# Cross-attention and routed experts on one core: softmax sums from ACT's accumulator in place of ones-matmuls

## The reference

```python
x = x + xattn(layernorm(x), ctx, ctx, mask, Wq, bq, Wk, bk, Wv, bv, Wo, bo)   # x, ctx: (8, 512, 512) fp32
x = x + ffn(layernorm(x), Ws, bs, W1, b1, W2, b2)

# xattn, 16 heads of 32
sim = einsum('bnid,bnjd->bnij', qh, kh) * 32 ** -0.5
sim = where(~mask[:, None, None, :], finfo.min, sim)
out = einsum('bnij,bnjd->bnid', softmax(sim, axis=-1), vh)      # then @ Wo + bo

# ffn: 8 experts, each takes the 512 tokens with the highest softmax(x @ Ws + bs)
h = gelu(einsum('ekd,edf->ekf', x[routes], W1) + b1)            # F = 2048
y = (einsum('ekf,efd->ekd', h, W2) + b2) * route_vals           # added back at routes
```

## Time and profile before

| | us |
|---|---|
| median of 3 runs | 1895.03 (1890.82 to 1898.14) |
| the profiled execution | 1893.99 |
| its span, first to last instruction | 1892.3 |
| TensorE busy (PE) | 1738.4 |
| VectorE busy (DVE) | 1145.1 |
| ScalarE busy (ACT) | 719.6 |
| GpSimd busy (POOL) | 459.2 |
| mean granted TensorE clock | 0.970 of full |

### The profile page before, as it was taken

One profiled execution on the slowest core, in us unless ns is written; L12 is line 12 of the kernel. 1 busy time (PEld: TensorE's weight loads), 2 busy tenths in 40 slices (PEclk: granted clock), 3 DMA queues, 4 the chain that ended last, 5 costly groups with the idle time before them and its releaser, 6 DMA issues.

```text
span 1892.3 us, 23403 instructions
## 1 busy us (share of the span) xinstructions
PE 1738.4 (92%) x8787; PEld 1171.3 (62%) x8787; DVE 1145.1 (61%) x1917; ACT 719.6 (38%) x1215; POOL 459.2 (24%) x730
## 2 busy tenths in 40 slices
PE   5799989989999999999899837999999999999996
PEld 4455645545546545455455325878888888888885
DVE  5576675775775865856766564777645454455543
ACT  3355454454554553543544511222223222222321
POOL 4332333323423323333333102010202020202001
PEclk9899999999999999999999957999999999999998
DMA  5232332323423323323323213243434242525331
GB/s 159 82 92 67 115 87 68 115 66 79 134 63 91 101 67 105 95 64 112 85 69 104 88 56 112 89 117 112 140 104 147 90 140 89 162 68 162 95 106 23
DMA packets 117289, 185.39 MB, mean 98 GB/s; under 512 B 24380, under 2 KB 58320, under 8 KB 117176
## 3 DMA queue, kind: packets, MB, share of 16 engines
q1 hardware_dynamic: 88312, 117.13, 19.5%
q0 software_dynamic: 28864, 66.75, 13.8%
HBM read 107.64 MB, written 25.31 MB: 70 GB/s over the span
## 4 chain that ended last, share of the span: by engine, by line
PE 76%; DVE 11%; issue 3%; DMA 3%; ACT 2%; SPq 2%; POOL 2%; ACTq 0%; POOLq 0%; DVEq 0%
PE ps_gen L635 8%; PE ps_gen L636 8%; PE ps_gen L637 8%; PE ps_gen L1643 6%; PE ps_gen L1645 6%; PE ps_gen L1644 6%; PE ps_den L1493 5%; PE ps_att L1493 5%; PE ps_gen L1465 5%; PE ps_gen L1479 4%; DVE maxes L1133 3%; PE ps_gen L1451 3%; PE ps_gen L1452 3%; PE ps_gen L1453 3%; DVE rden L1148 1%
## 5 line engine op out<-in xcount | busy, mean ns | idle before, releaser
L1133 DVE TENSOR_REDUCE maxes<-ps_gen 128x1 f32<-128x512 f32 x512 | 333.9, 675 | 203.0 <-PE ps_gen L1465 202.5
L948 ACT ACTIVATE p_ring<-ps_gen,keep_scale 128x512 f32<-128x512 f32 x512 | 331.8, 686 | 291.5 <-PE ps_gen L1479 291.2
L1350 DVE TENSOR_TENSOR gel_lo<-gel,gel_hi 128x512 fp32r<-128x512 f32 x126 | 87.2, 692 | 288.1 <-ACT gel_hi L1027 279.7
L1026 ACT ACTIVATE gel<-ps_gen,b_cols 128x512 f32<-128x512 f32 x128 | 88.3, 690 | 450.5 <-PE ps_gen L637 450.4
L1465 PE MATMUL ps_gen<-kst,qst 97*128 97x512 f32 x512 | 209.1, 428 | 23.0 <-issue 8.7
L1479 PE MATMUL ps_gen<-qst,kst 99*128 99x512 f32 x512 | 200.0, 436 | 17.6 <-DVE cT_lo L1083 9.0
L635 PE MATMUL ps_gen<-hT_hi,w_hi 128*128 128x512 f32 x512 | 203.0, 396 | 1.5 <-DVE hT_lo L1343 1.5
L636 PE MATMUL ps_gen<-hT_lo,w_hi 128*128 128x512 f32 x512 | 200.1, 391 | 0.0
L637 PE MATMUL ps_gen<-hT_hi,w_lo 128*128 128x512 f32 x512 | 200.1, 391 | 0.0
L1643 PE MATMUL ps_gen<-w_hi,gel_hi 128*128 128x512 f32 x504 | 198.1, 393 | 0.0
L895 POOL DMA_INDIRECT out_x<-y_out,idx x32 | 55.7, 1740 | 583.3 <-ACT y_out L1046 504.7
(11 more groups left out here) (199 smaller groups left out, 2778.4 us busy)
## 6 DMA issues: line engine op xcount, KB each, us to landing
w_raw<-in_L_ffn_W SPq DMA_DIRECT2D x128, 512.0 KB, 3.5
kst<-kT_hi POOLq DMA_DIRECT2D x256, 64.0 KB, 2.0
qst<-qT_hi SPq DMA_DIRECT2D x256, 64.0 KB, 2.0
x_in<-in_x POOLq DMA_DIRECT2D x60, 256.0 KB, 3.1
kst<-kT_lo POOLq DMA_DIRECT2D x128, 64.0 KB, 1.9
qst<-qT_lo SPq DMA_DIRECT2D x128, 64.0 KB, 2.0
out_x<-x_in SPq DMA_DIRECT2D x32, 256.0 KB, 2.0
hn_rows<-x_in SPq DMA_DIRECT2D x32, 256.0 KB, 2.1
```

Of the source, the lines that this page charges most:

```text
L948: e.activation(p_ring[n % NP_][:, :], ps("score", g, kt, h)[:, :], ACT.Exp, scale=keep_scale[:, b:b + 1]).then_inc(drained_sem("score", g, ...
L1133: e.reduce_max(maxes[:, h * TB + t:h * TB + t + 1], ps("max", g, h, t)[:, :], AX.X).then_inc(drained_sem("max", g, h, t), 1)
```

## The change

The softmax sums are made in another place. The max product of a tile is kept in its PSUM bank after DVE has taken its row extremes; ACT then takes exp(product - extreme) over the same tile, writes it back into the bank, and its accumulator output gives the row's sum in a column of `den` (step `sum`, 16 per group). The bank is free after that. So that the extreme can be ACT's bias, all is negated: Wq and its bias are multiplied by -SCALE when they are split, the products come out as the negated scaled scores, DVE takes a minimum into `nmax` (two buffers), and the exp has scale -1. `keep_scale` is 1 or 0 times -1.

The sums' way to the division: step `rden`, placed 0.02 into the next group: DVE reciprocal on 128x16, TensorE transpose to 16 rows, DVE copy into a part of `by_row`, a DMA of 8 KB on SP's queue to `rden_rows` in HBM; step `rden_in`, 0.3 into the next group: a DMA on SP's queue that reads it back with each head's row broadcast to 32 partitions, 256 KB into `rden_b`. DVE's `divide` multiplies `ps_att`, read in PSUM, by `rden_b`. The `den` steps, `ps_den`'s copies and the large reciprocals are gone; PSUM's eighth bank becomes a seventh `ps_gen`, which the search uses as `ps_den`. (Exp of the large product has the mask's row in it, as the scores have.)

The copies of V and route go from ACT to DVE. Of the table, V's products for the next batch are spread over one group's length from 0.36 of r3 on (`V_NEXT_AT`), the late work starts earlier and lasts 0.72 of a group for 0.52, and the context's loads are 0.1 of a group later. Waits on `s_av` count one step per kt where they counted two.

```diff
-NGEN = 6
+NGEN = 7
...
+    def max_of(self, g, h, t):
+        key = ("max", g, h, t)
+        self.with_bank(*key)
+        self.put_late(key, ("sum", g, h, t))
...
-    V_AT = (0.13, 0.33)
-    LOAD_C_AT, TURN_C_AT = (-0.1, 0.22), (0.5, 0.95)
+    RDEN_AT, RDEN_IN_AT = 0.02, 0.3
+    V_AT, V_NEXT_AT = (0.13, 0.33), (0.36, 1.36)
+    LOAD_C_AT, TURN_C_AT = (0.0, 0.32), (0.5, 0.95)
...
-    LATE_AT = (("residual", 0.15), ("add_bias", 0.38), ("out", 0.5), ("x1_norm", 0.61),
...
-    LATE_FOR = 0.52
+    LATE_AT = (("residual", 0.05), ("add_bias", 0.2), ("out", 0.3), ("x1_norm", 0.41),
...
+    LATE_FOR = 0.72
...
-            soon.extend([(a.add, "recip", g, n) for n in range(TB)] + [(a.add, "divide", g), (nothing,), (a.osplit, g)])
+            soon.extend([(a.add, "divide", g), (nothing,), (a.osplit, g)])
...
+                elif kind == "rden":
+                    g, = at
+                    on.wait_ge(*drained("rden", g))
+                    if g >= 2:
+                        on.wait_ge(s_rd_in, 16 * (g - 1))
+                    e.dma_start(rden_rows[g % 2].rearrange("h (t n) -> (h t) n", n=P), rd_rows).then_inc(s_rd_out, 16)
+
+                elif kind == "rden_in":
...
+                    src = rden_rows[g % 2].rearrange("h (r n) -> h r n", r=1).to_broadcast([HG, DH, S])
+                    e.dma_start(rden_b[:, :], src).then_inc(s_rd_in, 16)
...
-                    e.activation(w_hi[w][:, c, :], stage_of(w, c)[:, :], ACT.Copy).then_inc(s_w_hi, 1)
+                    e.activation(w_hi[w][:, c, :], stage_of(w, c)[:, :], ACT.Copy, scale=-SCALE if w == "q" else 1.0
...
+                elif kind == "sum":
+                    g, h, t = at
+                    c = slice(h * TB + t, h * TB + t + 1)
+                    psum = ps("max", g, h, t)
+                    on.wait_ge(s_min, (g * HG + h) * TB + t + 1)
+                    if g >= 2:
+                        on.wait_ge(s_rden, g - 1)
+                    e.activation(psum[:, :], psum[:, :], ACT.Exp, bias=nmax[g % 2][:, c], scale=-1.0, accum_out=den[g % 2][:, c]
+                                 ).then_inc(drained_sem("max", g, h, t), 1)
...
-                    e.activation(rden[:, :], ps_den[:, :], ACT.Copy).then_inc(s_nrm, 1)
-                    e.activation(att_n[:, :], ps_att[:, :], ACT.Copy).then_inc(s_nrm, 1)
...
-                    e.reduce_max(maxes[:, h * TB + t:h * TB + t + 1], ps("max", g, h, t)[:, :], AX.X
-                                 ).then_inc(drained_sem("max", g, h, t), 1)
+                    if g >= 2:
+                        on.wait_ge(*full("rows", g - 2))
+                        on.wait_ge(*drained("max", g - 2, HG - 1, TB - 1))
+                    e.tensor_reduce(nmax[g % 2][:, h * TB + t:h * TB + t + 1], ps("max", g, h, t)[:, :], AX.X, ALU.min
+                                    ).then_inc(s_min, 1)
...
+                    e.reciprocal(rden[:, :], den[g % 2][:, :]).then_inc(s_rden, 1)
+                    on.wait_ge(*full("rden", g))
+                    if g > 0:
+                        on.wait_ge(s_rd_out, 16 * g)
+                    e.tensor_copy(rd_rows, ps("rden", g)[0:HG * TB, 0:P]).then_inc(drained_sem("rden", g), 1)
...
+                    e.tensor_tensor(att_n[:, :], ps_att[:, :], rden_b[:, :], ALU.mult).then_inc(s_nrm, 1)
```

More of the change, by code:

```diff
@@ L310, in attention_agenda @@
             if before[0] >= 0:
[L311 removed]
+                attend(*before)
             fill(time[1])
[L313 to L314 removed]
             a.with_bank("score", i, kt, 2)
@@ L397, in attention_moe_kernel @@
         keep_scale = sb(p1, "keep_scale", [P, B])
-        maxes = sb(p1, "maxes", [P, HG * TB])
+        nmax = [sb(p1, f"nmax{i}", [P, HG * TB]) for i in range(2)]
+        den = [sb(p1, f"den{i}", [P, HG * TB]) for i in range(2)]
+        rden = sb(p1, "rden", [P, HG * TB])
         stat = [sb(p1, f"stat{i}", [P, 6]) for i in range(2)]
@@ L408, in attention_moe_kernel @@
         bias_rows = hnT[0:3 * DC, 2, :]
-        mask_neg = rden[0:B, :]
+        mask_neg = rden_b[0:B, :]
+        max_rows = [by_row[n * QUAD:n * QUAD + HG * TB, :] for n in range(2)]
+        rd_rows = raw(by_row[2 * QUAD:2 * QUAD + HG * TB, :])
         p1.close()
```

155 lines of the change are left out of this document (82 added, 73 removed).

## The result

The changed kernel takes 1959.6 us (median of 4 runs, 1948.4 to 1966.7); the kernel before took 1894.4 beside it. The ratio is 1.034, 95% interval 1.029 to 1.039: slower by 65 us, where 105 us less were forecast. The profiled execution is the shortest of the four and has a span of 1946.6 us; the two kernels differ by 54 us in their profiles.

The account below looks back on a forecast made before the run. TensorE was taken to bound attention. Seven batches at 13.5 us give 94.5, plus 4.7, 3.5 and 3.5 makes 106; 1894.0 - 106 + 1 = 1789 us, range 1757 to 1838.

Parts of the forecast that it names:

- A den step between other products takes 0.99 us ... 1.18 us ... 4.7 us per group: TensorE in attention: removing 128 ones-matmul steps at 1.18 us each saves 4.7 us per group, 151 us in all.
- the ones-matmuls were no bound: Rival, TensorE in attention: removed steps did not bound and the gain is eaten; 1894 us, from 1850 up; chance 0.04.
- The 45 us between those 151 and the forecast's 106: Whole kernel: den steps removed were priced at 151 us, but only 106 us of gain was forecast.
- r0: First of a batch's four kinds of group (four heads each): from 47.7 to 35.5 us, set by TensorE; ACT 24.
- r2: Third kind of group in a batch: from 24.35 to 23 us, ACT taking over from TensorE's 20.0.
- 1.1 us per batch for the banks held back: PSUM banks in attention: 1.1 of 14.6 us per batch kept back for max banks held by two instructions, leaving 13.5.
- I take 0.3 to 0.5 us each: TensorE early in the next group: wait for DVE at each of 32 added transposes of the reciprocals.
- It bounds nothing: DVE in attention: its busy time falls by 1 to 2 us per group and it limits no group.
- one fall per batch, 2.5 us, in a rival: Rival of held banks and clock: gaps lower TensorE's clock; with held banks, gain 7 us per batch, 1836 us; chance 0.14.
- nothing booked: Late work (residual to back), started earlier and spread wider: no cost counted, up to 3 us per batch for the range.
- r3: Fourth kind of group in a batch: from 25.8 to 29.7 us, TensorE gaining 8.3 us of V products.
- r1: Second kind of group in a batch: from 31.4 to 26.5 us, by TensorE with its 3.5 us idle kept.

Follow-up runs that it names:

- e13: Kernel before with three of four den steps (ones-matmuls) left out, nothing added or moved: 1861.6 us, ratio 0.982.
- e10: Changed kernel without ACT's sums and without the reciprocals' whole path, V and route copies back on ACT: 1814.7 us, ratio 0.957.
- e1: Changed kernel with rden moved from 0.02 to 0.3 of the next group and rden_in from 0.3 to 0.5: 1964.1 us, ratio 1.037.
- e6: Changed kernel with DVE's reciprocal left at 0.02, its transpose and copy moved to 0.25, the read to 0.45: 1956.6 us, ratio 1.033.
- e2: Changed kernel with only the route copies put back from DVE to ACT: 1944.0 us, ratio 1.026.
- e12: Changed kernel without ACT's sums and without the reciprocals' path, V and route copies staying on DVE: 1848.4 us, ratio 0.975.
- e7: Changed kernel with the old table's places for V, the context's loads and the late work: 2002.8 us, ratio 1.057.
- e16: Changed kernel with the sums' logarithm folded into the rows replacing the reciprocals' path, route copies on ACT, maxima, logarithm and rows placed earlier: 1909.1 us, ratio 1.007.

## Why the prediction was wrong

- **"A den step between other products takes 0.99 us ... 1.18 us ... 4.7 us per group": the first step that failed.** As work it was nearly right: 128 to 137 us of 151 left TensorE's account. As path it was not: with nothing added, 96 of the steps are worth 34 us and not 113 (e13), 0.35 us each. The argument was that TensorE, busy 94% of the stretch in rows 2, is the bound, so that what goes from it goes from the time. But 94% busy does not say how far the other chains are behind: at the place shown the stacks' chain already ended 0.64 us after TensorE did, so nothing of the step could come off there. The waits that grew in e13 are of three kinds (maxima 16 us, max products 11, layer norm 8.5), and the lower clock took 25 to 31 us more. The rival "the ones-matmuls were no bound" had 0.04, dismissed by those same 94%.
- **The 45 us between those 151 and the forecast's 106, for everything that was added: the second step that failed, and by more.** Sums, path and copies on DVE cost 145 us (e10 against the changed kernel). The prediction summed them as busy time per engine (24 of 35.5 us for ACT in r0), with 3 us in r2 for ACT and 1.1 us per batch for the banks held back. The runs show waits between the engines in place of that; the next two points are the parts that can be named.
- **"I take 0.3 to 0.5 us each" for the reciprocals' transpose: mis-sized.** It waited 57.8 us in 23 times, 2.5 us each. The row that it was sized by, the wait for the maxima, is a wait behind a max product; here DVE had the layer norm of two tiles ahead in the stop shown. But this wait alone is not the loss (e1, e6).
- **The route copies on DVE were costed as busy time only.** The logits wait for them, 35.9 us in 20 times; the engine of these copies is worth 16 us in e2, that of V's and route's together 34 us between e12 and e10. "It bounds nothing" was right for DVE's busy time (57% of the span, 1099.9 us where 1060 to 1090 was forecast) and wrong for its answers.
- **The clock was booked as one fall per batch, 2.5 us, in a rival.** It cost 59 to 69 us more than before in attention, some 8 per batch.
- **The late work's "nothing booked"** can't be told apart; its table as a whole helps (e7).
- **Right:** the sum's 0.66 us (0.64); ACT's 984 us (about 1000); the expert stage's 742 us; r3 nearly, 31.7 for 29.7. TensorE's busy time was to fall by about 135 us and fell by 68, to 1670.3: most of the work went, but what is left runs at the lower clock for longer. r2, of which ACT was to take over, is 25.7 us on average for 23, but ACT is busy 80% of it, not over 90. The misses are r0, 45.1 for 35.5, and r1, 35.7 for 26.5, which were priced by TensorE's work alone: 37.61 x 0.92 = 34.6 us of it is in that r0, very near the 35.5, and the other 10 us are idle time and lower clock.

The ledger in runs: before 1894; den and its copies gone and the table new, with nothing in den's place and the copies of V and route on ACT, 1815 (e10), -80 where -151 was read off; those copies on DVE 34 more, 1848 (e12); sums and path 111 more, 1960. The forecast was off by 171 us. 71 of them are in the price of what was removed (151 for 80), and 100 in what was added (45 for 145). So the den step is not the whole of the miss, and not its larger part; with it alone put right the forecast would still have been a gain, of 35 us.

**What stays open.** Which chain holds r2 at 24 to 25 us with every load off is not shown: in e10 its idle time is put down to "issue", as at the place above, and to the minima, but no run shortened the stacks' 12 DMAs, and what makes the maxima late in e13, the largest part of its new idle time, was not followed. How the 111 us of sums and path divide is open too, since each costs 64 when added alone, and gives back 45 to 48 when taken out alone. For the sums, ACT's time and the held banks are not told apart.

## What to carry to other kernels

A busy share of 94% doesn't make an engine's instructions worth their length: before pricing a removed step, look at the engine's next wait behind it, and whether what that wait is for moves too; if it does not, the step's time comes back as waiting. When four engines hand each other tiles in fixed orders, a new hand-over has to be costed by what stands in the answering engine's queue at that place, not by its own length. And a large wait in a list is no gain until a run without it shows one: 56 us of waits taken away left the time where it was (e6), and 44 us brought 7 (e16).
